# One clamp of the WKV exponent on GpSimd, one-product values in every third job, and new engine orders

## What is computed

```
x = x + rwkv(LN(x))        # 4 layers
x = x + ffn(LN(x))         # blockwise FP4 quantized gate, up and down products, 128 -> 352 -> 128
x = x + attention(LN(x))   # one head of 64, causal
x = x + ffn(LN(x))         # the same FP4 block again

# one rwkv layer
h  = LN(x); hh = time_shift(h)
xk, xv, xr = h*tm + hh*(1-tm)            # one tm vector for each
k, v, sr = xk@Wk.T, xv@Wv.T, sigmoid(xr@Wr.T)
x = x + (sr * wkv(w, u, k, v)) @ Wo.T    # a scan over tokens
x = x + sigmoid(..@Wcr.T) * (square(relu(..@Wck.T)) @ Wcv.T)
# a step of wkv, with pp the running maximum exponent and w = -exp(time_decay)
ww2 = pp + w; qq2 = max(ww2, kk)
e1b = exp(ww2 - qq2); e2b = exp(kk - qq2)
aa, bb, pp = e1b*aa + e2b*vv, e1b*bb + e2b, qq2
```

## Time and profile before

| | |
|---|---|
| device time, median of 3 runs | 1396.85 us (1396.58 to 1397.21) |
| profiled execution, span | 1396.8 us |
| TensorE busy | 1311.6 us, 94% |
| ScalarE busy | 1261.8 us, 90% |
| VectorE busy | 1250.5 us, 90% |
| GpSimd busy | 1160.8 us, 83% |

### The profile page before, as it was taken

One profiled execution on the slowest core, in us unless ns is written; L12 is line 12 of the kernel. 1 busy time (PEld: TensorE's weight loads), 2 busy tenths in 40 slices (PEclk: granted clock), 3 DMA queues, 4 the chain that ended last, 5 costly groups with the idle time before them and its releaser, 6 DMA issues.

```text
span 1396.8 us, 23610 instructions
## 1 busy us (share of the span) xinstructions
PE 1311.6 (94%) x7285; PEld 929.9 (67%) x7285; DVE 1250.5 (90%) x2169; ACT 1261.8 (90%) x2533; POOL 1160.8 (83%) x1218
## 2 busy tenths in 40 slices
PE   3699999999999999999999999999999999999997
PEld 1356667666666666676666677766667777667776
DVE  6999999999999999999999999579999467789994
ACT  6799999999999999999999999767777889888874
POOL 6888999999998999998998999969998445467983
PEclk9999999999999999999999999999999999999999
DMA  7000000000000000000000000100000000000011
GB/s 232 0 1 1 1 1 1 1 20 13 1 1 1 1 1 1 1 1 1 1 2 0 1 1 9 31 24 23 24 1 1 1 1 1 1 8 23 24 31 38
DMA packets 26924, 18.55 MB, mean 13 GB/s; under 512 B 1072, under 2 KB 26160, under 8 KB 26800
## 3 DMA queue, kind: packets, MB, share of 16 engines
q1 hardware_dynamic: 26800, 17.05, 4.2%
HBM read 12.85 MB, written 4.19 MB: 12 GB/s over the span
## 4 chain that ended last, share of the span: by engine, by line
ACT 40%; PE 30%; issue 11%; POOL 10%; DVE 8%; DMA 0%; ACTq 0%; SPq 0%; POOLq 0%; DVEq 0%
ACT z L757 10%; ACT kf L867 6%; PE ps L1211 5%; ACT kf L874 3%; PE ps L1190 3%; ACT rc L841 3%; PE ps L1152 3%; ACT ed L818 3%; PE ps L1183 3%; PE ps L1261 3%; PE ps L1135 3%; ACT er L835 2%; PE ps L1243 2%; ACT ed L819 2%; ACT ed L830 2%
## 5 line engine op out<-in xcount | busy, mean ns | idle before, releaser
L1152 PEld LDWEIGHTS ps<-W,kf 128*128 128x128 f32 x2048 | 245.9, 193 | 33.1 <-issue 32.3
L1135 PE MATMUL ps<-xk,W 128*128 128x512 f32 x512 | 262.5, 595 | 1.0 <-DVE xk L404 0.9
L1152 PE MATMUL ps<-W,kf 128*128 128x128 f32 x2048 | 251.2, 276 | 0.0
L757 ACT ACTIVATE z<-X,ln_rs 128x128 f32<-128x128 f32 x512 | 219.2, 720 | 6.1 <-POOL ln_rs L606 6.1
L867 ACT ACTIVATE kf<-ps 128x512 f32<-128x512 f32 x256 | 210.8, 823 | 3.5 <-PE ps L1135 3.5
L874 ACT ACTIVATE kf<-kf 128x1024 f32<-128x1024 f32 x128 | 164.7, 1287 | 0.0
L1040 PEld LDWEIGHTS ps<-idn,z 128*128 128x128 f32 x664 | 81.1, 143 | 113.7 <-issue 68.4
L1040 PE MATMUL ps<-idn,z 128*128 128x128 f32 x664 | 101.9, 277 | 32.8 <-ACT z L757 19.4
L604 POOL TENSOR_TENSOR ln_rs<-ln_rs,mhalf 128x8 f32<-128x8 f32 (+1 forms) x70 | 122.9, 1756 | 0.0
L707 POOL TENSOR_TENSOR W<-W,hsc 128x704 f32<-128x704 f32 x64 | 88.9, 1389 | 30.3 <-DVE hsc L482 30.3
L666 POOL TENSOR_TENSOR p<-p,rc 128x512 f32<-128x512 f32 x64 | 104.2, 1628 | 8.6 <-DVE p L381 8.0
(11 more groups left out here) (178 smaller groups left out, 4041.5 us busy)
## 6 DMA issues: line engine op xcount, KB each, us to landing
X<-x_in SPq DMA_DIRECT2D x16, 256.0 KB, 6.8
xi<-x_in SPq DMA_DIRECT2D x16, 256.0 KB, 2.8
out<-X SPq DMA_DIRECT2D x16, 256.0 KB, 2.3
W<-weights SPq DMA_DIRECT2D x4, 832.0 KB, 8.4
W<-fp4w SPq DMA_DIRECT2D x1, 560.0 KB, 3.6
row<-rows SPq DMA_DIRECT2D x1, 192.0 KB, 2.9
wqkv<-qkv SPq DMA_DIRECT2D x1, 96.0 KB, 5.9
idn<-ident SPq DMA_DIRECT2D x1, 64.0 KB, 3.0
```

Of the source, the lines that this page charges most:

```text
L757: last = e.activation(chunk(dst, j), chunk(src, j), ACT.Identity, bias=rs[:, 1, j:j + 1], scale=rs[:, 0, j:j + 1])
L1135: e.matmul((pF0, pF1)[f % 2][:, :], w_of(r, WCK + f), xk[r % 2][:, :], start=True, stop=True).then_inc(kf_mm[f], 1)
L1152: last = e.matmul(chunk(pKV, j), kf[r % 3][:, f, j * 128:(j + 1) * 128], w_of(r, WCV + f), start=f == 0 and j == 0, stop=f == 3, skip_grou ...
```

## The change

Four things are changed.

1. `args` is split. ScalarE keeps relu(d + ew) as `arg_old`. GpSimd gets `clamp_new`: one TENSOR_SCALAR that writes min(d, -ew), bounded below by a large negative number, over 128x512. `exp_k` on ScalarE then reads this with a bias of ew and no scale.
2. In layers 2 to 4 each job whose number is divisible by 3 (16 jobs of 64: 18, 21, ... 63) gets its v token mixed by VectorE in `mix_v`, into two free parts of `big`, and `values` makes one product. The other jobs of these layers still make two, now of the shifted `h` and of `dh1`. Layer 1 is as before. The weight preparation of layers 2 to 4 has one VectorE instruction less per layer.
3. The lists of steps of all four engines have a new order and new offsets.
4. The second FFN starts 23 ticks after the first one rather than 28, the attention 15 rather than 16, and the first FFN at tick `NR + 6` rather than `NR + 5`.

```diff
-FFN_AT = NR + 5
+FFN_AT = NR + 6
-GAP = 12
-ATT_AT, FFN2_AT, TICKS = FFN_AT + NB, FFN_AT + NB + GAP, FFN_AT + 2 * NB + GAP + 18
+ATT_AT, FFN2_AT = FFN_AT + 15, FFN_AT + 23
+TICKS = FFN2_AT + 35
...
+        xv = [big[:, 2 + k, :] for k in range(2)]
+        one_v = lambda r: r >= NB and r % 3 == 0
+        v_mixes = lambda r: sum(one_v(k) for k in range(r))
...
+            def mix_v(r):
+                if 0 <= r < NR and one_v(r):
+                    w.wait_ge(v_mm, r - 1)
+                    w.wait_ge(dh1_done, r + 1 - EARLY)
+                    e.scalar_tensor_tensor(out=xv[r % 2], in0=dh1[r % 2][:, :], scalar=v_of(r, TMV), in1=h1[r % 3][:, 0:T],
+                                           op0=ALU.mult, op1=ALU.add).then_inc(xv_done, 1)
...
+            def clamp_new(r):
+                if 0 <= r < NR:
+                    w.wait_ge(wneg_done, 1)
+                    w.wait_ge(s1_done, r - 1)
+                    w.wait_ge(bb_done, r - 1)
+                    w.wait_ge(d_done, r + 1)
+                    e.tensor_scalar(ed[r % 2][:, 1, :], dd[r % 2][:, :], col(wneg, r), -FAR, ALU.min, ALU.max).then_inc(new_done, 1)
...
-            def args(r):
+            def arg_old(r):
                 if 0 <= r < NR:
                     w.wait_ge(wneg_done, 1)
-                    w.wait_ge(s1_done, r - 1)
-                    w.wait_ge(bb_done, r - 1)
                     w.wait_ge(d_done, r + 1)
-                    e.activation(ed[r % 2][:, 0, :], dd[r % 2][:, :], ACT.Relu, bias=col(ew, r))
-                    e.activation(ed[r % 2][:, 1, :], dd[r % 2][:, :], ACT.Relu, bias=col(wneg, r), scale=-1.0).then_inc(args_done, 1)
+                    e.activation(ed[r % 2][:, 0, :], dd[r % 2][:, :], ACT.Relu, bias=col(ew, r)).then_inc(old_done, 1)
...
-                    w.wait_ge(args_done, r + 1)
-                    e.activation(ed[r % 2][:, 1, :], ed[r % 2][:, 1, :], ACT.Exp, scale=-1.0).then_inc(ek_done, 1)
+                    w.wait_ge(new_done, r + 1)
+                    e.activation(ed[r % 2][:, 1, :], ed[r % 2][:, 1, :], ACT.Exp, bias=col(ew, r)).then_inc(ek_done, 1)
...
-                    e.matmul(pV[:, :], w_of(r, WV), h1[r % 3][:, 1:T + 1], start=True, stop=False)
-                    e.matmul(pV[:, :], w2_of(r), h1[r % 3][:, 0:T], start=False, stop=True).then_inc(v_mm, 1)
...
+                    elif one_v(r):
+                        w.wait_ge(xv_done, v_mixes(r + 1))
+                        e.matmul(pV[:, :], w_of(r, WV), xv[r % 2], start=True, stop=True).then_inc(v_mm, 1)
+                    else:
+                        w.wait_ge(h1_done, r + 1)
+                        w.wait_ge(dh1_done, r + 1 - EARLY)
+                        e.matmul(pV[:, :], w_of(r, WV), h1[r % 3][:, 0:T], start=True, stop=False)
+                        e.matmul(pV[:, :], w2_of(r), dh1[r % 2][:, :], start=False, stop=True).then_inc(v_mm, 1)
```

More of the change, by code:

```diff
@@ L546, in vector @@
-                mix_k(t - 10)
                 fh_max(ffn_job(t - 6))
+                a_mask(att_job(t - 6), 0)
+                fx_max(ffn_job(t - 2))
+                fh_scale(ffn_job(t - 6))
+                add_xa(t - 8)
                 fh_add(ffn_job(t - 7), 1)
-                prepare(t - 4)
-                fh_scale(ffn_job(t - 6))
+                mul_s1(t - 6)
+                fh_inverse(ffn_job(t - 6))
+                scan_bb(t - 6)
                 fh_sub(ffn_job(t - 7), 1)
-                a_mask(att_job(t - 6), 0)
@@ L579, in vector @@
                 sub_d(t - 5)
+                rwkv(t - 7)
+                bn2(t - 8)
+                mix_v(t - 4)
+                a_bn(att_job(t - 2))
+                a_max(att_job(t - 6), 1)
+                fx_scale(ffn_job(t - 2))
+                bn1(t - 2)
+                a_mask(att_job(t - 6), 2)
+                a_max(att_job(t - 6), 2)
+                weights_rounded(t - Q_AT - 4)
+                arg_r(t - 5)
+                init_stats(t)
+                a_mask(att_job(t - 6), 3)
@@ L586, in gpsimd @@
+                mul_up(ffn_job(t - 5), 2)
+                mix_rt(t - 4)
+                mix_r(t - 10)
+                weights_scales(t - Q_AT + 2)
+                prepare(t - 1)
+                mul_up(ffn_job(t - 5), 3)
+                mul_rv(t - 5)
         def gpsimd():
@@ L986, in scalar @@
             for t in range(TICKS):
+                a_exp(att_job(t - 7), 1)
+                fx_magic(ffn_job(t - 4))
+                norm1(t - 4)
+                relu(t - 11, 0)
+                a_exp(att_job(t - 7), 2)
+                init_z(t - 2)
+                keep_ax(att_job(t - 5))
+                a_exp(att_job(t - 7), 3)
+                keep_hq(ffn_job(t - 9), 2)
+                silu(ffn_job(t - 6), 1)
+                relu(t - 11, 1)
+                square(t - 12, 1)
+                keep_fx(ffn_job(t - 5))
@@ L987, in scalar @@
+                keep_h2(t - 10)
+                arg_old(t - 6)
+                fh_magic(ffn_job(t - 7), 0)
+                tanh_c(t - 12)
+                weights_out(t - Q_AT - 15)
+                silu(ffn_job(t - 6), 2)
                 silu(ffn_job(t - 6), 3)
+                seeds(t - 7)
                 put_x(ffn_job(t - 9))
-                tanh_c(t - 12)
+                exp_k(t - 6)
+                f_z(ffn_job(t - 2))
+                relu(t - 11, 2)
+                exp_r(t - 6)
                 keep_hq(ffn_job(t - 8), 0)
-                seeds(t - 7)
+                keep_h1(t - 4)
```

232 lines of the change are left out of this document (101 added, 131 removed).

## The result

The changed kernel takes 1424.41 us (median of 4 runs, 1421.68 to 1426.39); the kernel before took 1396.71 in the same session (4 runs, 1395.51 to 1397.21). The ratio is 1.0196, with a 95% interval of 1.0181 to 1.0212: slower by 27.7 us, where 15.9 us less was forecast.

A forecast was written before the change was run, and what follows sets the result against it. TensorE and ScalarE were taken as both full at a 13.20 us tick. A 12.95 us tick over 48 jobs wins 12 us, the tail 4: 1396.8 - 12 - 4 = 1380.8, predicted 1381 us, range 1366 to 1392.

The forecast's parts named there:

- What bounds the kernel now: rwkv part: TensorE and ScalarE both full at a 13.20 us tick, so freeing one of the two alone gives nothing.
- ScalarE: rwkv tick: second relu leaves, 0.61 us less, exp_k's bias adds 0.09; from 13.20 to 12.68 us.
- TensorE: Layers 2 to 4: 16 of 48 jobs lose one 0.86 us product, 0.29 a tick on the mean; 12.91 us.
- `mix_v` is the same operation on the same shapes as `mix_rt`, whose slot is 0.66: VectorE, layers 2 to 4: a third of 0.66 us, 0.22, added to 12.72 us a tick makes 12.94.
- the clamp at 0.80: GpSimd, rwkv tick: 12.28 us plus 0.80 makes 13.08, or 12.67 if scaled_p is relieved; middle taken, 12.88.
- the point of decision: GpSimd, rwkv tick: a clamp over 0.92 us puts GpSimd past today's 13.20 us period; named as a sign of being wrong.
- Light and heavy jobs even out: Layers 2 to 4: ticks with mix_v (VectorE 13.38) and the others (TensorE 13.20) average to 12.95 us.
- The rest of the rwkv part at 0: Layer 1, where TensorE keeps both products, stays near 13.2 us a tick or longer; no gain counted.
- The tail, 4 won: Attention and second FFN share four more ticks: 0.9 us won, plus 3 from a new order with fewer TensorE waits.
- The eight added table loads: Tail, ScalarE: 10.3 us, priced within the 17.36 us shared tick; a rival (14%) had them on the path, 1391 us.
- GpSimd becomes the bound: Rival, 10%, slower: the clamp takes more than 0.92 us of an rwkv tick; 1414 us, or 1400 at 1.04.
- the tick sticks while no engine is full: Sign of being wrong, rwkv part: the tick stays at 13.2 us though no engine is full.

The follow-up runs named there:

- e5_before_clamp: Kernel before, with only the clamp put on GpSimd and exp_k given the bias: 1401.68 us, where the kernel before took 1398.47 in that session.
- e8_pairs: In place of the kernel, VectorE and GpSimd run series of one instruction each over 128x512, alone and side by side: 186.47 us for the one run.
- e4_both_moved: Changed kernel with mix_t and mix_v both moved behind arg_r in VectorE's order: 1397.14 us, ratio 1.0001 to the kernel before.
- e1_no_mixv: Changed kernel with no v token mixed by VectorE, so values makes two products in every job: 1402.32 us, ratio 1.0038.
- e2_mixv_moved: Changed kernel with mix_v alone moved three VectorE instructions later, behind arg_r: 1405.45 us, ratio 1.0061.
- e9: e4_both_moved with rwkv moved ahead of sub_d on VectorE: 1449.54 us, ratio 1.0361.
- e10: e4_both_moved with gate and rwkv both moved behind bn1 on VectorE: 1443.27 us, ratio 1.0314.
- e11: e4_both_moved with rwkv alone moved behind bn1, ahead of arg_r, on VectorE: 1436.3 us, ratio 1.0271.

## Why the prediction was wrong, point by point

- **What bounds the kernel now** was read nearly rightly: two engines were full, but freeing ScalarE alone does give 0.11 us a tick (e5_before_clamp). What the list of bounds lacked is a resource with no column of its own, the access to SBUF that VectorE and GpSimd exclude each other from. From e8_pairs and the slots of a tick I estimate its use in the changed kernel: GpSimd's large instructions take 5 x 1.23 + 2 x 1.00 + 0.66 = 8.8 us; VectorE's with all inputs in SBUF are four mixes at 0.66, `rwkv` and `gated` at 0.60 and `arg_r` at 0.40, 4.2 us. Together that is 13.0, and 13.7 with `mix_v`. A whole tick is 13.2. It is an estimate, and too high for a bound: the pair's 1.63 for 1.89 shows that some of it overlaps, and e4_both_moved has light ticks of 12.70 and 12.86.
- **ScalarE** was right: `exp_k` has a slot of 0.61 us, and over 33 whole ticks (238.20 to 687.75) it was busy for 423.23 us, 12.83 a tick for the 12.68 forecast.
- **TensorE** at 12.91 can't be confirmed: over the same ticks it was busy for 13.17 each, and for 12.97 in e4_both_moved, and busy time is not need. It was not what failed: with VectorE relieved (e4_both_moved), ticks with both products take 12.70 to 12.86, under the 13.20 of before. This fits a saving that spreads over light and heavy jobs, though e5_before_clamp shows that 0.11 of it was free without any product less.
- **VectorE: "`mix_v` is the same operation on the same shapes as `mix_rt`, whose slot is 0.66". This step failed.** The slot is 502.81 - 501.37 = 1.44 us. And `mix_t`, whose move to `scan_pp` was priced at nothing, has 513.42 - 512.21 = 1.21 for its 0.78 of before, in every tick. The price was taken from the right form in the wrong company. The term was 12.94 us and is 13.62; a third of `mix_v`'s excess of 0.78 and `mix_t`'s of 0.43 are 0.69 of these 0.68. e1_no_mixv and e2_mixv_moved put 22.1 and 19.0 us on `mix_v`'s presence and place; e4_both_moved returns 27.3 of 27.7 by the place of two instructions.
- **GpSimd: the clamp at 0.80.** It is 0.66 us alone and 501.31 - 500.36 = 0.95 in place. The size is within the bounds given, past the 0.92 that I named as the point of decision, and yet GpSimd did not become the bound: it was busy for 12.71 us a tick for the 12.88 forecast. `scaled_p` was relieved, 1.27 for 1.72, as hoped, but `add_xb` was stretched in its place, 1.74 for 1.27. By e5_before_clamp the clamp costs 3 us of the kernel before. The 2.5 cycles for two inputs that the prediction puts in section 3.1 of the Trainium skill's GPSIMD Engine Reference stand in its section 2.1; section 3.1 has 2.6, an estimate of 1.11 us, under the 1.22 that the add of e8_pairs took.
- **"Light and heavy jobs even out"** failed for the same cause. A full engine evens out nothing: the heavy ticks are longer by 14.51 - 13.18 = 1.33 us, which is `mix_v`'s slot of 1.44 less the 0.11 by which `arg_r` is spared beside it. The two-deep buffers even out TensorE's load, not VectorE's.
- **The rest of the rwkv part at 0** failed too: the first 16 jobs lost 4.1 us, of which the cause is open, and the tick that rounds the FP4 weights takes 19.41 where it took 16.63, since `mix_rt` and `mix_r` are stretched in it (1.76 and 1.75). The prediction has no term for that tick. The weight instruction less in each layer was not tried.
- **The tail, 4 won,** was about right at an equal clock. From the last `scan_pp` to the end 1.6 are won in the changed kernel and 6.0 in e4_both_moved (533.8 for 539.8), but the granted clock there was 0.98 in the kernel before and in the changed one, and 0.99 in e4_both_moved. Between the last `ham` of either FFN, where the kernel before and e4_both_moved had 1.00, it is 289.74 for 1371.14 - 1077.30 = 293.84, so 4.1 won: 1.6 by the four shared ticks, where 0.9 was forecast, and 2.5 by the orders and the rest, where it was 3. The 17.36 of the earlier trace rows was taken as the price of a shared tick. It was the longest of the old kernel's four (from 1197.63 to 1262.27, 16.16 on the mean), and the added ones cost 17.8; the win comes from what they replace, which costs 18.24. The eight added table loads are there (22 in all), and no longer tail came of them.
- **The rivals.** The loss came on the side of "GpSimd becomes the bound", with its lock, but not by its path. I weighed the rule on GpSimd's rows alone ("the many unstretched rows fit less"). Those rows are unstretched where VectorE reads PSUM or where VectorE was the one held back; the place to look was VectorE's own rows, and the engine at 96.37% is the one that cannot pay. The announced sign "the tick sticks while no engine is full" did not come either: VectorE looked full.

How many of VectorE's stretches are left in e4_both_moved, and whether some order of both engines together gives less than its 13.03, stays open; only orders of VectorE alone were tried.

## What to carry to other kernels

Price an instruction of VectorE or GpSimd by its form, its operands' places and what the other engine runs at that moment; sum the SBUF-only work of VectorE and the large operations of GpSimd as one more engine, as a warning and not as a bound. A busy share of 100% may be partly waiting: compare the rows of one form across a tick, and the longest against the shortest tells how much. When reordering one engine to dodge another, draw both: an instruction that is spared ends sooner, and what follows it meets someone else.

## What was not expected of the hardware

The one who starts first is spared even by a margin of 0.06 us (`sub_dh` at 501.31, `mix_v` at 501.37), so small shifts change which engine pays: three moves of one or two instructions (e9, e10, e11) cost 39 to 52 us over e4_both_moved. A TENSOR_SCALAR of VectorE with one SBUF input is held as well (median 1480 ns beside adds, 907 beside clamps, where alone 16 took 6.42 us):

```profile
L36 DVE TENSOR_SCALAR dv<-da,cola x14: 475/1480/1589, 141.5 to 156.8; 128x512 f32<-128x512 f32 x14
```

BN_STATS, which also has one SBUF input, did not stretch beside the clamp, nor the clamp beside it (1.41 for four and 0.69, in e11). GpSimd's clamp of 128x512 took 0.66 us, little more than half its two-input add.
